# A decoder layer in fp32 pairs on one core: a gate, a column sum, weight splits, residual shifts and one normalisation unit change places at the start of the feed-forward part

## The reference, cut to what matters

```python
x = _layernorm(x + attention(x))
x = _layernorm(x + cross_attention(x, ctx))
amp = sigmoid(x @ amp_w + amp_b)
ph = tanh(x @ ph_w + ph_b) * pi
h = (cos(ph) + sin(ph)) * amp
for l in range(2):
    e = h @ ent_w[l] + ent_b[l]
    h = _layer_norm(h + e @ ent_pw[l] + ent_pb[l], ln3_g[l], ln3_b[l])
    t = einsum('bsd,pdf->pbsf', h, path_w[l]) + path_b[l][:, None, None, :]
    mod = cos(phase[l]) + sin(phase[l])
    h = _layer_norm(h + sum(t * mod), ln4_g[l], ln4_b[l])
x = _layernorm(x + h)        # x is 8 x 256 x 512
```

## Time and profile before

| | |
|---|---|
| median of 3 runs | 908.25 us (907.48 to 910.91) |
| the profiled execution's own time | 908.9 us |
| its span | 907.1 us |
| mean granted TensorE clock over the span | 0.978 of 2.4 GHz |
| PE busy | 852.8 us (94%) |
| DVE busy | 707.3 us (78%) |
| ACT busy | 533.6 us (59%) |
| POOL busy | 390.9 us (43%) |

### The profile page before, as it was taken

One profiled execution on the slowest core, in us unless ns is written; L12 is line 12 of the kernel. 1 busy time (PEld: TensorE's weight loads), 2 busy tenths in 40 slices (PEclk: granted clock), 3 DMA queues, 4 the chain that ended last, 5 costly groups with the idle time before them and its releaser, 6 DMA issues.

```text
span 907.1 us, 18841 instructions
## 1 busy us (share of the span) xinstructions
PE 852.8 (94%) x5696; PEld 714.2 (79%) x5696; DVE 707.3 (78%) x2069; ACT 533.6 (59%) x1561; POOL 390.9 (43%) x657
## 2 busy tenths in 40 slices
PE   6899999999899999999999998997989999999992
PEld 5778888888787888888888887775778788788881
DVE  5778888888878878797787887877877677678576
ACT  6656566566666757575756655784534553751752
POOL 4456645465766656454654521415015005104205
PEclk9999999999999999999999999997999999999997
DMA  6655454544494846575584648530102002000001
GB/s 200 220 166 158 131 150 154 173 143 141 168 269 132 269 134 210 154 236 142 168 232 132 189 116 263 212 126 24 47 0 94 1 1 80 14 1 36 12 1 46
DMA packets 79712, 116.68 MB, mean 129 GB/s; under 512 B 8976, under 2 KB 42768, under 8 KB 78992
## 3 DMA queue, kind: packets, MB, share of 16 engines
q1 hardware_dynamic: 76032, 112.02, 39.9%
q10 hardware_dynamic: 3600, 3.68, 1.3%
HBM read 57.46 MB, written 17.31 MB: 82 GB/s over the span
## 4 chain that ended last, share of the span: by engine, by line
PE 52%; DVE 9%; ACT 4%; issue 3%; SPq 2%; POOL 2%; DMA 1%; DVEq 0%; POOLq 0%; ACTq 0%
PE bank L161 24%; PE bank L2243 12%; PE bank L1525 4%; PE bank L2276 4%; PE bank L1511 2%; PE bank L1548 2%; PE bank L1552 1%; DVE stats L2117 1%; SPq L700 1%; ACT prob L1107 1%; DVE w_ffn L1843 1%; DMA xres<-in_x 1%; PE bank L1466 1%; DVE wave L1757 1%; DVE xT L2062 0%
## 5 line engine op out<-in xcount | busy, mean ns | idle before, releaser
L1107 ACT ACTIVATE prob<-bank,nmax 128x128 f32<-128x128 f32 (+1 forms) x512 | 209.7, 433 | 24.2 <-DVE nmax L1271 21.8
L1271 DVE CUSTOM_DVE_ANT_0 bank<-bank,mask 128x128 f32<-128x128 f32 (+1 forms) x512 | 167.8, 384 | 3.5 <-DVE cv L1202 2.3
L2243 PE MATMUL bank<-hT,w_ffn 128*128 128x512 f32 x576 | 140.4, 399 | 0.7 <-ACT hT L2007 0.3
L2243 PEld LDWEIGHTS bank<-hT,w_ffn 128*128 128x128 f32 x576 | 108.6, 191 | 27.7 <-ACT hT L2007 1.9
L918 POOL TENSOR_TENSOR zone<-raw,zone 128x256 fp32r<-128x256 f32 x128 | 97.8, 797 | 58.5 <-ACT zone L1054 58.5
L1525 PE MATMUL bank<-ident,prob 128*128 128x128 f32 x768 | 119.6, 278 | 1.7 <-DVE stage L1180 1.1
L1120 ACT ACTIVATE probT<-bank 128x512 f32<-128x512 f32 x97 | 58.4, 603 | 98.7 <-PE bank L1552 98.5
L1107 ACT ACTIVATION_READ_ACCUMULATOR prob<-bank,nmax 128x1 f32 x512 | 111.4, 218 | 0.0
L161 PE MATMUL bank<-xT,w_q 128*128 128x256 f32 x768 | 102.0, 285 | 2.4 <-DVE o L1292 2.3
L161 PEld LDWEIGHTS bank<-xT,w_q 128*128 128x128 f32 x768 | 98.3, 191 | 7.2 <-issue 2.3
L1511 PE MATMUL bank<-k,q 96*128 96x128 f32 (+1 forms) x512 | 99.5, 298 | 2.2 <-ACT prob L1107 0.9
(11 more groups left out here) (177 smaller groups left out, 1519.4 us busy)
## 6 DMA issues: line engine op xcount, KB each, us to landing
q<-stage SPq DMA_DIRECT2D x192, 128.0 KB, 2.7
k<-kstage SPq DMA_DIRECT2D x48, 256.0 KB, 3.9
x<-xres SPq DMA_DIRECT2D x16, 512.0 KB, 4.4
raw<-in_ent_wT SPq DMA_DIRECT2D x32, 256.0 KB, 4.0
raw<-in_ent_pw SPq DMA_DIRECT2D x32, 256.0 KB, 4.3
raw<-in_path_w SPq DMA_DIRECT2D x8, 512.0 KB, 3.7
xres<-in_x SPq DMA_DIRECT2D x8, 512.0 KB, 4.0
x1b<-x SPq DMA_DIRECT2D x8, 512.0 KB, 4.7
```

The source lines that it names most:

```text
L1107: ins = s.activation(prob[:, u, c * width:(c + 1) * width], banks[u][:, c * width:(c + 1) * width], ACT.Exp, scale=-1.0, bias=nmax[:, i % ...
L1271: ins = v.tensor_tensor_reduce(scored, scored, mask[:, S - width:S], scale=-1.0, scalar=3e38, op0=ALU.add, op1=ALU.min, accum_out=nmax[:, ...
L2243: ins = t.matmul(banks[plan.bank((f"z{s_}", n))][:, :], W[s_][:, a, c * D + n * P:c * D + (n + 1) * P], hT[:, h, c, :], start=c == 0 and a ...
```

## The change

1. Flush, step 1, on DVE: `gate(3)` stands ahead of `stage_lo(v, 1)`.
2. Block 0, on DVE: `stage_lo(v, 2)` leaves the start of the block for the gap of layer 0, and the two halves of `stage_lo(v, 3)`, which stood in the gaps of layers 0 and 1, become one whole in the gap of layer 1. `stored(v)` stands behind `column_centred(0)`.
3. Block 0, on PE: `column_total(0)` moves from behind c = 1 to behind c = 2 of layer 0.
4. On POOL: the eight residual pieces of block 0 and `residual_of_path(3)` move from the start of the feed-forward part into the flush: four pieces at the end of step 0, four at the start of step 1, and `residual_of_path(3)` right behind them, ahead of the two `rstd_of` of the last attention rows.
5. Block 0, on DVE: the four `x2T_lo` move from in front of `unit(0)` to behind it.
6. The small tiles `c` and `c_sum` become part of the tile `cols`. The semaphore `s_res` is made elsewhere.

```diff
@@ attention, gpsimd, body(t)
                     if i == 0 and t.after == "self":
                         split_x()
+                    if t is flush and i == 1:
+                        for n in range(BT, 2 * BT):
+                            ffn.residual(g, 0, *divmod(n, 2))
+                        ffn.residual_of_path(g, 3, ident)
                     for name in t.fillers(i):
                         if name[0] in ("wo", "wout"):
                             rstd_of(name)
...
                     if t is last_cross and i == NG - 1:
                         ffn.residual_of_path(g, 1, ident)
+                    if t is flush and i == 0:
+                        g.wait_ge(ffn.s_ln, 32)
+                        g.wait_ge(ffn.s_xb0, 16)
+                        pr.wait_full(g, last_cross, ("xt", BT - 1))
+                        for n in range(BT):
+                            ffn.residual(g, 0, *divmod(n, 2))
@@ attention, vector, body(t)
                     if t is flush and i == 1:
+                        gate(3)
                         ffn.stage_lo(v, 1)
-                        gate(3)
                         v.wait_ge(s_os, t.lin(NG))
                         v.wait_ge(s_fd[KT], 16 * NL)
@@ class FeedForward
-        small = sb(whole, "cols", [P, N_COLS + KT + TURNED * KT + 1])
+        small = sb(whole, "cols", [P, N_COLS + KT + TURNED * KT + 1 + TURNED * KT + 1])
...
+    def residual(self, g, b, i, half):
+
+        own = self.xb[b % 2][:, i, half * D // 2:(half + 1) * D // 2]
+        g.tensor_tensor(own, own, self.lnb[:, half * D // 2:(half + 1) * D // 2], ALU.add).then_inc(self.s_res, 1)
...
-    def stage_lo(self, v, n, pieces=range(KT)):
+    def stage_lo(self, v, n):
 
-        for c in pieces:
+        for c in range(KT):
@@ feed-forward, gpsimd
-            ffn.residual_of_path(g, 3, ident)
-            g.wait_ge(ffn.s_ln, 32)
-            g.wait_ge(ffn.s_xb0, 16)
-            g.wait_ge(s_h0lo, 1)
-            for n in range(2 * BT):
-                residual(0, *divmod(n, 2))
@@ feed-forward, vector, body
                 if b == 0:
-                    ffn.stage_lo(v, 2)
-                    stored(v)
                     column_sum(0)
                     ffn.bias_partials(v, 3)
                     column_centred(0)
+                    stored(v)
                     v.tensor_copy(ffn.ones_r[:, :], ffn.ones[:, :])
...
                     if b == 0:
-                        ffn.stage_lo(v, 3, range(2 * s_, 2 * s_ + 2))
+                        ffn.stage_lo(v, 2 + s_)
...
-                if b == 0:
-                    for i in range(BT):
-                        x2T_lo(k, i, b * BT + (i + 1))
                 for i in range(BT):
                     unit(i)
+                    if b == 0 and i == 0:
+                        for u in range(BT):
+                            x2T_lo(k, u, u + 1)
@@ feed-forward, tensor, body
                     if b == 0 and c == 0:
                         column_sum(0)
-                    if b == 0 and c == 1:
+                    if b == 0 and c == 2:
                         column_total(0)
```

More of the change, by code:

```diff
@@ L1599, in gate_products @@
                           lambda h, c: xT[:, :, h, c, :], range(KT))
[L1602 to L1606, removed]
 LAYERS = 2 * NL
@@ L1643, in __init__ @@
         self.A, self.s_passed = A, s_passed
-        small = sb(whole, "cols", [P, N_COLS + KT + TURNED * KT + 1])
+        small = sb(whole, "cols", [P, N_COLS + KT + TURNED * KT + 1 + TURNED * KT + 1])
         self.cols, self.path_bias = small[:, 0:N_COLS], small[:, N_COLS:N_COLS + KT]
-        self.row_mean, self.eps = small[:, N_COLS + KT:N_COLS + KT + TURNED * KT], small[:, N_COLS + KT + TURNED * KT:]
+        at = N_COLS + KT + TURNED * KT
+        self.row_mean, self.eps = small[:, N_COLS + KT:at], small[:, at:at + 1]
+        self.c = small[:, at + 1:at + 1 + TURNED * KT].rearrange("p (s k) -> p s k", s=TURNED)
+        self.c_sum = small[:, at + 1 + TURNED * KT:]
         self.half_ampb = sb(whole, "half_ampb", [P, KT])
@@ L1675, in __init__ @@
         self.centres = sb(over, "centres", [P, BT])
-        self.c = sb(over, "c", [P, TURNED, KT])
-        self.c_sum = sb(over, "c_sum", [P, 1])
         self.var2, self.rstd2 = sb(over, "var2", [P, BT]), sb(over, "rstd2", [P, BT])
@@ L1695, in __init__ @@
         self.s_h0hi, self.s_h0lo = sem("s3_h0hi"), sem("s3_h0lo")
+        self.s_res = sem("s3_res")
     def constants(self, g):
@@ L1883, in ffn_phase @@
     s_bn, s_agg, s_var, s_rstd = sem("s3_bn"), sem("s3_agg"), sem("s3_var"), sem("s3_rstd")
-    s_res = sem("s3_res")
     s_cen, s_sum, s_shift, s_scaled = sem("s3_cen"), sem("s3_sum"), sem("s3_shift"), sem("s3_scaled")
@@ L1934, in gpsimd @@
         def gpsimd(g):
-            def residual(b, i, half):
-                at = slice(half * D // 2, (half + 1) * D // 2)
-                g.tensor_tensor(xb[b % 2][:, i, at], xb[b % 2][:, i, at], lnb[:, at], ALU.add).then_inc(s_res, 1)
-            ffn.residual_of_path(g, 3, ident)
-            g.wait_ge(ffn.s_ln, 32)
-            g.wait_ge(ffn.s_xb0, 16)
-            g.wait_ge(s_h0lo, 1)
-            for n in range(2 * BT):
-                residual(0, *divmod(n, 2))
             def body(b, plan, last):
@@ L1975, in body @@
                     for n in range(2 * BT):
-                        residual(b + 1, *divmod(n, 2))
+                        ffn.residual(g, b + 1, *divmod(n, 2))
             every_block(g, body)
@@ L2154, in finish @@
                     v.wait_ge(s_rstd, b * LN + number[b][i])
-                    v.wait_ge(s_res, 2 * n)
+                    v.wait_ge(ffn.s_res, 2 * n)
                     v.wait_ge(s_cen, n)
```

## The result

The changed kernel takes 895.42 us (median of 3 runs, 895.34 to 896.65) against 908.25 us: a ratio of 0.9856, 95% interval 0.9822 to 0.9890. It is faster by 12.8 us. The forecast was 899.0, the range 896.3 to 902.0: right in sign, 0.9 us outside the range. The profiled execution took 896.65 us, its span is 894.8.

The account below looks back on a forecast made before the run. PE, busy nearly throughout, was taken as the bound, with gains where it waits or runs at its lower clock. 7.5 - 0.2 + 2.0 = 9.3 us off 908.9 gives 899.6; median 0.65 lower: 899.0, range 896.3 to 902.0.

Parts of the forecast that it names:

- lateness s from POOL's pieces: Flush: eight POOL pieces beside DVE delay the start of DVE's queue from gate(3) on by 1.8 us.
- `gate(3)` and `stage_lo(1)`: DVE's queue in the flush ahead of L1860: the gate takes 2.0 us, the four staging pieces 2.8.
- the first place: PE's 6.62 us wait for the column total and lower clock behind it; removal gains 7.5 us, DVE becoming the bound.
- lost in layer 1's gap: Two more stage_lo pieces on DVE, 1.4 us, behind a wait for ACT of 1.22: 0.2 us lost.
- the second place: PE's 2.55 us wait for mm3's bank, slow matmuls behind it; unit(0) earlier gains 2.0 of 3.9 us.
- PE's gap ahead of layer 1: New wait of PE, 1.8 us, from 624.1 to the first high part, 1.45 behind DVE's copy.
- gaps ahead of `ph0`, `amp0`: New PE waits for the banks of mm1 and mm2 at the second place: 0.4 and 1.4 us.
- Rival 3: Clock falls in a new PE gap: 900.0 at layer 0, 900.5 at the gates, 901.5 both; chance 0.20.
- rivals 4 to 6: Nothing gained, 904 to 910 (0.06); weight 3 late on POOL, slower (0.03); layer 1's longer gap fully on path, 900.2 (0.03).
- rival 1: Little contention from POOL's pieces in the flush: s = 0.5, 1.3 us more gained, 897.7; chance 0.16.
- the one point where the Trainium skill was weighed: DVE beside POOL: the skill's rule of full blocking would add both durations; the prediction took a milder price, 0.45 us a piece.
- the scatter: Whole execution: the range allowed 0.9 us for the scatter of runs; the median was taken 0.65 below the single execution.

Follow-up runs that it names:

- experiment 6: The changed kernel without the eight residual pieces in the flush (last bias not added to the first 512 rows): 895.92 us, ratio 0.9887, region 100.68.
- experiment 4: The unchanged kernel with unit(0) ahead of the four x2T_lo (part 5) alone: 904.55 us, ratio 0.9974, region 110.12.
- experiments 9 and 10: Changed kernel with stage_lo(2) back at block 0's start, 899.23 us; with mm0 to mm2 read early, 898.13; bias_partials(3) in DVE's flush waits, 895.79; last two together, 896.70.
- experiments 3 to 5: The unchanged kernel with part 6 (the tile) alone, 906.48 us; with part 5 alone, 904.55; the changed kernel without part 5, 897.96.
- experiments 6 to 8: Changed kernel without the eight residual pieces, 895.92 us; with part 4 undone, 901.94; with stage_lo(1) ahead of gate(3) again (part 1 undone), 898.61.
- experiments 7 and 9: Changed kernel with POOL's residual back at the feed-forward part's start (part 4 undone), 901.94 us; with stage_lo(2) back at block 0's start, 899.23.
- experiment 5: The changed kernel without part 5 (the four x2T_lo again ahead of unit(0)): 897.96 us, ratio 0.9896, region 104.06.

## Why the prediction was right, and where it was wrong

| step of the prediction | forecast | measured |
|---|---|---|
| lateness s from POOL's pieces | 1.8 | 1.36; by experiment 6, 1.40 |
| `gate(3)` and `stage_lo(1)` | 2.0 + 2.8 | 4.40 |
| L1860 (now L1870) to the copy | 4.05 | 4.15 |
| gain at the first place | 7.5 | 8.3 |
| lost in layer 1's gap | 0.2 | 0.26 |
| gain at the second place | 2.0 | 2.4; alone (experiment 4) 2.1 |
| sum for the region | 9.3 | 10.3 |
| rest of the span | 0 | 0.2 |
| PE's gap ahead of layer 1 | 1.8 | 0.39, and 0.63 ahead of layer 0 |
| gaps ahead of `ph0`, `amp0` | 0.4, 1.4 | 0.59, 0.97 |

**The mechanisms held.** Both waits went, DVE became the bound at the first place, POOL's pieces cost part of the gain, the second gain was cut by two new gaps, and the gap of layer 1 cost next to nothing. The clock stayed at 1.00, so the 2.9 us and 1.5 us lost behind the old waits came back in full. Rival 3 (clock) and rivals 4 to 6 did not happen. For rival 3 that says little: the gap of 1.8 us that it was about did not come, the longest new gap being 0.97. The result lies below the 897.7 of rival 1 too, but the rows do not show that rival: s was 1.36, not 0.5. `residual_of_path(3)` was done 4.6 us before anybody needed POOL.

**Terms of the sum that were mis-sized.** Three, all on the cautious side, 1.2 us together. Small terms the other way (4.15 for 4.05, 0.26 for 0.2, and 0.1 more from the first copy to the copies of layer 1) leave 1.0. First s, forecast at 1.8, was 1.36. The error lies with the four pieces of step 0. Timeline of DVE before, the same instructions without POOL beside them:

```profile
589.56 0.47 DVE L1798 TENSOR_SCALAR xb<-w_raw,cols 128x512 f32<-128x512 f32 x1
590.14 2.47 DVE L1801 SCALAR_TENSOR_TENSOR xb<-w_raw,cols,xb 128x512 f32<-128x512 f32 x3
```

Beside POOL they took 1.04 and 3.33 us, and the first `h0` (592.21, not slowed itself) came 1.36 us later behind the arrival; up to 1.8 was forecast. DVE's idle 0.84 went, and 0.41 was left at `stage_lo(0)` (594.98) in place of 0.9. Step 1's four pieces added 0.95, forecast 0.9. POOL's own pieces went at 0.98 and 1.05 us, not 1.17. On the one point where the Trainium skill was weighed (SBUF — State Buffer, Who interferes with whom) the runs decide against adding the durations: DVE's work from L1808 to the first `h0` takes 3.05 us alone and four POOL pieces at 0.725 2.90, 5.95 together, but with both at work it was done in 4.42 (587.79 to 592.21). Second, `stage_lo(1)` took 2.49 us; I had taken the pace of L1845, 0.70, from another form of instruction, where L1843 (now L1853) without POOL beside it goes at 2.49 / 4 = 0.62. From its start at 615.39 to L1870 at 617.80 it is 2.41 for 2.8: 0.4. The gate took its 2.0. Third, the second place. There `unit(2)` stood 4.07 us behind `unit(1)`, not 4.28: 0.2 of the 0.4.

PE's gap ahead of layer 1 was forecast at 1.8 and is 0.39. Of the 1.4 between them, 0.7 is the copy that comes sooner, and 0.63 is the gap ahead of layer 0, which the prediction did not have: it left PE's own start where it was. The profile names no releaser for that gap, but the record shows it to be a wait for DVE. PE's queue stands there until the banks of the last attention rows are read (`wait_all`, L1591 of the changed kernel), which the second L1321 does. In all nine profiles with a gap ahead of layer 0, PE starts 1.00 or 1.01 us behind the start of that L1321 (611.01 behind 610.00). In experiment 6 L1321 starts at 609.10 and PE is busy past 610.11, so the gap is gone.

**The step that failed is the last one, the scatter.** With 10.3 in place of 9.3 the forecast would have been 898.0, and 895.42 is 2.6 us below that: 1.8 from the arrival, 0.2 from the rest, and 0.6 because the median lies 1.23 us below the profiled run's own time and not 0.65. The prediction made the sum against one profiled execution and allowed 0.9 us for the scatter of runs. Sixteen profiles with the same instructions up to the flush arrive there between 585.25 and 588.91 us:

| profile | arrival | region |
|---|---|---|
| unchanged, three profiles | 588.50, 585.63, 585.84 | 112.43, 112.25, 112.07 |
| changed, three profiles | 586.74, 585.75, 586.83 | 102.11, 102.08, 101.94 |
| the other ten kernels | 585.25 to 588.91 | |

The region repeats within 0.4 us, the part ahead of it only within 3.7. The first profile of the kernel before was one of the three latest. The medians of three runs carry this scatter too: 908.25 for the unchanged kernel, where the later sessions gave 907.72, 906.52, 907.10 and, in the session of experiments 9 and 10, 906.70; 895.42 for the changed one, where they gave 895.65 and 896.14. The differences of medians are 12.8, 12.1 and 11.0 us; the interval of every ratio holds the 10.3 us of region and rest (averages 10.2 and 0.1; 0.9887). The other kernels show that such a surplus goes with the session. In that of experiments 3 to 5 their medians differ from the unchanged kernel's by 0.9 to 1.5 us more than their regions and rests account for, in that of experiments 6 to 8 by 1.1 to 1.9 us less, though these three have the changed kernel's code ahead of the flush. So about 2 of the 12.8 us are most likely not the change's. A margin of 2 us and more on either side, in place of 0.9, would have held the result.

What makes the arrival scatter stays open. PE's waits for the split of the next input ahead of the flush (L861 as releaser) were 4.8 us in the first profile of before and 3.6 in that of after, but 3.5 in the latest of all (588.91). Stretches at the lower clock come at 25 to 30, 51 to 58, 242 to 249 and 560 to 566 us, in some executions and not in others, but the earliest arrival (585.25) has the last two of them. Whether the changed kernel has a small real share in this is not excluded: its medians lie 0.7 and 1.8 us lower than region and rest account for.

## What to carry to other kernels

Make the sum of a change against a stretch that repeats (from a mark before the changed code to one behind it), and give the rest of the span its own margin from several profiles or, if there is only one, a wide one. When a wait of the busiest engine is removed, write down the queue of the engine that is late next, piece by piece. That told here in advance that the first place would give 7.5 us (8.3 were measured) and not the 9.9 that PE alone would allow. A gain handed to the next block is kept only if the engines that feed it come sooner as well: 2.6 us won before the second block were 2.1 us of new waits in it.

## What the runs showed of the hardware

**The clock behind an idle.** Behind idles of 3.02 and 2.36 us (experiments 7 and 9) 12 matmuls took 4.58 and 4.45 us in place of 3.0. Behind the 2.55 or 2.56 us ahead of `mm3` they took 4.31 to 4.61 in four profiles and 3.04, at a granted clock of 1.00, in the fifth (experiment 5). Behind 1.95 to 1.98 us at about 560 us they took 4.33 to 4.59 in 14 of the 16 profiles and 3.01 and 3.02 in two, one of each kernel. Nothing fell behind 1.10, 0.97 or 0.63. So the length of one idle alone does not tell it. In the region each of these falls cost about 1.5 us, and the one behind the 6.62 cost 2.9.

**A late feeder can cost more than it is late.** Experiments 7 and 9 delayed DVE by 2.3 and 2.6 us, and the region grew by 3.8 and 4.1: PE's gap grew to 3.02 and 2.36 us, and the lower clock behind it took another 1.6 and 1.5.

**POOL beside DVE.** Pieces of 128x256 on POOL beside DVE's 128x512 slowed DVE from 0.83 to 1.11 us an instruction on L1811, and from 0.69 to 1.22 on L1762 (598.69). All eight cost the path 1.40 us, since part of them fell into DVE's waits.
